# P times V in turns of three quarters behind every third softmax tile, in a fused attention and FP4-feed-forward layer on one core

## The reference

```python
qkv = (x @ w_qkv + b_qkv).reshape(b, n, 3, H, DH).transpose(2, 0, 3, 1, 4)
q, k, v = (qkv[0], qkv[1], qkv[2])
...
attn = jnp.einsum('bhqd,bhkd->bhqk', q, k) * scale
attn = jax.nn.softmax(attn, axis=-1)
out = jnp.einsum('bhqk,bhkd->bhqd', attn, v)
```

## Time and profile before

| | |
|---|---|
| median of 3 runs | 3654.96 us (3651.85 to 3660.76) |
| the profiled execution's own time | 3661.47 us |
| its span, first to last instruction | 3659.7 us |
| mean granted TensorE clock | 0.97 |
| TensorE matmul busy | 3412.5 us |
| VectorE busy | 3367.8 us |
| ScalarE busy | 2629.5 us |
| GpSimd busy | 911.9 us |

### The profile page before, as it was taken

How to read it: one execution, slowest core, us unless ns; L and a number is a source line. 1 busy time by engine, 2 the same in 40 slices (tenths; PEclk the granted TensorE clock), 3 DMA queues, 4 the chain that set the end, 5 groups by cost and what they waited for, 6 DMA issues and landing times.

```text
span 3659.7 us, 69024 instructions
## 1 busy us (share of the span) xinstructions
PE 3412.5 (93%) x27752; PEld 1539.9 (42%) x27752; DVE 3367.8 (92%) x3565; ACT 2629.5 (72%) x4870; POOL 911.9 (25%) x995
## 2 busy tenths in 40 slices
PE   7668999999999999999999999999999969999997
PEld 4343333333333333333333333333333336666665
DVE  8898999999999989999999999999999739999997
ACT  4342888888888888888888888888888833333333
POOL 6881000010000000000000000000000028888887
PEclk9885999999999999999999999999999989999999
DMA  5442112221211111111111111111111111211110
GB/s 162 144 168 89 57 66 72 74 69 65 73 57 47 55 61 67 58 41 43 50 61 61 59 61 48 41 41 62 63 67 52 46 42 46 79 42 39 40 34 21
DMA packets 134508, 230.63 MB, mean 63 GB/s; under 512 B 29510, under 2 KB 84006, under 8 KB 121894
## 3 DMA queue, kind: packets, MB, share of 16 engines
q1 hardware_dynamic: 124972, 217.82, 17.6%
q10 hardware_dynamic: 9216, 8.39, 0.7%
HBM read 156.33 MB, written 68.16 MB: 61 GB/s over the span
## 4 chain that ended last, share of the span: by engine, by line
PE 81%; DVE 9%; ACT 3%; issue 3%; DMA 1%; POOL 1%; SPq 1%; ACTq 0%; POOLq 0%; DVEq 0%
PE ps L625 36%; PE ps L678 32%; PE ps L758 7%; PE ps L768 4%; DVE arena L980 2%; DVE arena L985 1%; PE ps L728 1%; ACT arena L842 1%; PE ps L665 1%; ACT arena L851 1%; DVE arena L973 1%; DVE arena L1003 1%; ACT arena L889 0%; DMA qst<-qk_parts 0%; ACT v_all L899 0%
## 5 line engine op out<-in xcount | busy, mean ns | idle before, releaser
L1003 DVE TENSOR_REDUCE arena<-ps 128x1 f32<-128x1024 f32 x2048 | 2495.0, 1222 | 120.8 <-PE ps L625 103.9
L851 ACT ACTIVATE arena<-ps 128x512 f32<-128x512 f32 x4096 | 2226.1, 597 | 364.6 <-PE ps L665 280.0
L625 PE MATMUL ps<-kst,qst 48*128 48x512 f32 x4096 | 1522.1, 452 | 26.5 <-DMA qst<-qk_parts 22.2
L665 PE MATMUL ps<-qst,kst 51*128 51x512 f32 x4096 | 1494.4, 448 | 0.0
L678 PE MATMUL ps<-arena 128*32 128x256 f32 x16384 | 1312.2, 393 | 71.1 <-ACT arena L842 67.2
L625 PEld LDWEIGHTS ps<-kst,qst 48*128 48x128 f32 x4096 | 615.4, 188 | 886.0 <-DVE arena L1003 716.2
L678 PEld LDWEIGHTS ps<-arena 128*32 128x32 f32 x16384 | 326.7, 108 | 797.5 <-issue 459.8
L1259 POOL TENSOR_TENSOR arena<-arena,ones 128x16 bf16<-128x16 f32 x64 | 14.2, 221 | 2432.6 <-DVE arena L1008 2432.6
L665 PEld LDWEIGHTS ps<-qst,kst 51*128 51x128 f32 x4096 | 606.6, 185 | 11.1 <-ACT arena L851 7.7
L768 PE MATMUL ps<-wdT,arena 128*128 128x256 f32 (+1 forms) x768 | 195.0, 407 | 48.5 <-ACT arena L889 46.2
L899 ACT ACTIVATE v_all<-ps 128x352 f32<-128x352 f32 x128 | 59.3, 463 | 239.1 <-PE ps L758 238.9
(11 more groups left out here) (104 smaller groups left out, 2223.9 us busy)
## 6 DMA issues: line engine op xcount, KB each, us to landing
qk_parts<-arena SPq DMA_DIRECT2D x32, 1024.0 KB, 7.4
kst<-qk_parts SPq DMA_DIRECT2D x128, 256.0 KB
qst<-qk_parts SPq DMA_DIRECT2D x128, 256.0 KB
kst<-qk_parts SPq DMA_DIRECT2D x128, 128.0 KB
qst<-qk_parts SPq DMA_DIRECT2D x128, 128.0 KB
att<-arena SPq DMA_DIRECT2D x256, 34.0 KB
arena<-in_xT SPq DMA_DIRECT2D x16, 512.0 KB, 8.2
arena<-in_x SPq DMA_DIRECT2D x32, 256.0 KB
```

Source lines behind the costliest of these rows:

```text
L625: mm = nc.tensor.matmul(ps[:, i % S_BANKS, :], q[SROW:SROW + STACK, qt * P:(qt + 1) * P], k[SROW:SROW + STACK, kc * CHUNK:(kc + 1) * CHUNK ...
L665: nc.tensor.matmul(ps[:, bank_of_t(g.c, i), :], kst[g.u % 2][first:first + ROWS, kb * P:(kb + 1) * P], qst[g.u % 2][first:first + ROWS, qb ...
L851: nc.scalar.activation(pt[kb % 2][:, qb * CHUNK:(qb + 1) * CHUNK], ps[:, bank_of_t(g.c, i), :], ACT.Exp).then_inc(p_ready, 1)
L1003: nc.vector.tensor_reduce(mx[g.u % 2][:, i // 2, i % 2:i % 2 + 1], ps[:, bank:bank + 2, :].rearrange("p b t -> p (b t)"), AX.X, ALU.max).t ...
```

## The change

P times V is cut into quarters of 128 columns per block. Behind every third T tile (counted over all heads) come three quarters, sometimes four, or what is left of a head; a table `BEHIND` is made once by `products_behind`. Quarters of one block that stand together are one instruction per column group. `pt` gets a third buffer. ScalarE's copy of a head's output goes behind the exponential of the tile that its last quarters stand behind (`ENDS`), and `m_tile` goes behind tile 51, 52 or 53, the one that ends a run of three. S tiles are counted one by one. Where a run of three ends between the two S tiles of a pair, VectorE takes one maximum per bank (two reduces of 128 x 512) in place of one over both. The maxima of a head then need 4 columns per 128 queries in place of 2, and GpSimd sets them to the lowest float before each use.

```diff
-M_AFTER = 51
-
-HALF_AFTER = (1, 3)
+RUN, TILES_BACK = 3, 2
+QUARTERS, QUARTER = 4, 128
+
+MANY = 7
+
+P_BUFS = 3
+LOWEST = -3.4028234663852886e38
+
+M_FROM = 51
...
+def products_behind():
+
+    behind, done, head = {}, 0, KT * QUARTERS
+    for tile in range(G * TILES_S):
+        last_head = tile >= (G - 1) * TILES_S
+        if tile % RUN != RUN - 1 and not last_head or last_head and tile % CHUNKS != CHUNKS - 1:
+            continue
+        waiting = QUARTERS * max(0, (tile - TILES_BACK + 1) // CHUNKS) - done
+        count = waiting if last_head else min(waiting, QUARTERS if waiting >= MANY else QUARTERS - 1)
+        count = min(count, (done // head + 1) * head - done)
+        if count > 0:
+            behind[tile] = range(done, done + count)
+            done += count
+    return behind, range(done, G * head)
+
+
+BEHIND, AT_THE_END = products_behind()
+
+ENDS = {last.stop // (KT * QUARTERS) - 1: tile for tile, last in BEHIND.items() if last.stop % (KT * QUARTERS) == 0}
+
+
+def parted(g, pair):
+
+    beside = (g - 1) * TILES_S + 2 * pair - AHEAD
+    return beside >= 0 and beside % RUN == RUN - 1
+
+
+def m_after(g):
+
+    return M_FROM + (RUN - 1 - g * TILES_S - M_FROM) % RUN
...
-        mx = [take(KT * 2, "p (q c) -> p q c", c=2) for _ in range(2)]
+        mx = [sb(f"mx{i}", [P, KT, CHUNKS])[:, :, :] for i in range(2)]
...
-        pt = [take(N) for _ in range(2)]
+
+        pt = [take(N) for _ in range(P_BUFS - 1)] + [carve(12 * CHUNK + 16 * CHUNK)(N)]
...
-                pair = i // 2
                 if i == 0:
                     pe.wait_ge(s_in[g.u % 2], g.quad(128, 64 * (g.u // 2 + 1)))
-                if i % 2 == 0 and not (g.static(0) and pair < 2):
-                    pe.wait_ge(s_done, g.times(PAIRS, pair - 1))
+                wait_after(pe, s_done, g.times(TILES_S, i - S_BANKS + 1))
...
-                if i % 2:
-                    mm.then_inc(s_psum, 1)
+                mm.then_inc(s_psum, 1)
...
+            def pv(quarters):
+
+                g, first = divmod(quarters.start, KT * QUARTERS)
+                if first == 0:
+                    pe.wait_ge(v_staged, g + 1)
+                    wait_after(pe, o_out, g)
+                pe.wait_ge(p_ready, CHUNKS * ((quarters.stop - 1) // QUARTERS + 1))
+                at = quarters.start
+                while at < quarters.stop:
+                    block, q = divmod(at, QUARTERS)
+                    n = min(quarters.stop - at, QUARTERS - q)
+                    cols = slice(q * QUARTER, (q + n) * QUARTER)
+                    for qb in range(CHUNKS):
+                        mm = nc.tensor.matmul(ps[32 * qb:32 * qb + 32, O_BANK, cols], vs[g % 2][:, block % KT, :],
+                                              pt[block % P_BUFS][:, qb * CHUNK + cols.start:qb * CHUNK + cols.stop],
+                                              start=(block % KT == 0 and q == 0), stop=(block % KT == KT - 1 and q + n == QUARTERS))
+                    at += n
+                    if q + n == QUARTERS:
+                        mm.then_inc(pv_step, 1)
...
-                        halves = [HALF_AFTER.index(qb)] if qb in HALF_AFTER else []
-                        if g.static(G - 1):
-                            halves = [0, 1] if qb == CHUNKS - 1 else []
-                        for half in halves:
-                            if kb:
-                                pv(g, kb - 1, half)
-                            elif not g.static(0):
-                                pv(g.back(1), KT - 1, half)
+                        if g.c * TILES_S + kb * CHUNKS + qb in BEHIND:
+                            pv(BEHIND[g.c * TILES_S + kb * CHUNKS + qb])
...
-                    wait_after(act, pv_step, g.times(KT, kb - 1))
+                    wait_after(act, pv_step, g.c * KT + kb - P_BUFS + 1)
...
-                        if not g.static(0) and kb == 1 and qb == 0:
+                        if not g.static(0) and g.c * TILES_S + i == ENDS[g.c - 1]:
                             out_of_psum(g.back(1))
-                        if i == M_AFTER and not g.static(G - 1):
+                        if i == m_after(g.c) and not g.static(G - 1):
                             maxima(g.c + 1)
...
             def maxima(g):
+                dve.wait_ge(mx_clear, g.c + 1)
                 for i in range(PAIRS):
                     bank = 2 * i % S_BANKS
-                    dve.wait_ge(s_psum, g.times(PAIRS, i + 1))
-                    nc.vector.tensor_reduce(mx[g.u % 2][:, i // 2, i % 2:i % 2 + 1],
-                                            ps[:, bank:bank + 2, :].rearrange("p b t -> p (b t)"), AX.X, ALU.max
-                                            ).then_inc(s_done, 1)
+                    qt, kc = i // 2, i % 2 * 2
+                    if parted(g.c, i):
+                        for t in range(2):
+                            dve.wait_ge(s_psum, g.times(TILES_S, 2 * i + t + 1))
+                            nc.vector.tensor_reduce(mx[g.u % 2][:, qt, kc + t:kc + t + 1], ps[:, bank + t, :], AX.X, ALU.max
+                                                    ).then_inc(s_done, 1)
+                    else:
+                        dve.wait_ge(s_psum, g.times(TILES_S, 2 * i + 2))
+                        nc.vector.tensor_reduce(mx[g.u % 2][:, qt, kc:kc + 1],
+                                                ps[:, bank:bank + 2, :].rearrange("p b t -> p (b t)"), AX.X, ALU.max
+                                                ).then_inc(s_done, 2)
                     if i == PAIRS - 1:
-                        dve.wait_ge(s_done, g.times(PAIRS, i + 1))
+                        dve.wait_ge(s_done, g.times(TILES_S, TILES_S))
                         nc.vector.tensor_reduce(nm[g.u % 2], mx[g.u % 2], AX.X, ALU.max, negate=True).then_inc(neg_max, 1)
...
+            def clear_maxima(p):
+                nc.gpsimd.memset(mx[p], LOWEST).then_inc(mx_clear, 1)
...
                 p, first = g.u % 2, 3 * g.c
                 pool.wait_ge(neg_max, g.c + 1)
+                clear_maxima(p)
```

More of the change, by code:

```diff
@@ L140, in run_straight @@
                 fn(At(0, s - lag))
+def products_behind():
[18 more added lines that the diff above has]
+    return M_FROM + (RUN - 1 - g * TILES_S - M_FROM) % RUN
 def t_place(g, i):
-    return 1 + g * (TILES_S + 1) + i + (i > M_AFTER)
+    return 1 + g * (TILES_S + 1) + i + (i > m_after(g))
 def m_place(g):
-    return 0 if g == 0 else 1 + (g - 1) * (TILES_S + 1) + M_AFTER + 1
+    return 0 if g == 0 else 1 + (g - 1) * (TILES_S + 1) + m_after(g - 1) + 1
 def t_bank(place):
@@ L251, in layer_kernel @@
         bqk = take(4)
-        phase_a_end = arena_words - 2 * (2 * KT + 4 * KT)
+        phase_a_end = arena_words - 2 * 4 * KT
         WIDTHS = (6 * C, 6 * C, 2 * FF)
@@ L326, in layer_kernel @@
             "rot_ready", "rotsin", "t1_done", "qr_done", "hi_done", "parts_ready"))
-        s_psum, s_done, neg_max, m_step, m_split = (sem(n) for n in ("s_psum", "s_done", "neg_max", "m_step", "m_split"))
+        s_psum, s_done, neg_max, m_step, m_split, mx_clear = (sem(n) for n in (
+            "s_psum", "s_done", "neg_max", "m_step", "m_split", "mx_clear"))
         mt_psum, mt_out, t_psum, p_ready = (sem(n) for n in ("mt_psum", "mt_out", "t_psum", "p_ready"))
@@ L484, in head @@
                 if g < G - 2:
-                    sp.wait_ge(s_psum, bm * (8 * PAIRS) + (c + 1) * PAIRS)
+                    sp.wait_ge(s_psum, bm * (8 * TILES_S) + (c + 1) * TILES_S)
                     load_s(bm_s, (c + 2) % 8)
@@ L636, in t_bank_free @@
                 g, i = divmod(back - 1, TILES_S + 1)
-                if back == 0 or i == M_AFTER + 1:
+                if back == 0 or i == m_after(g) + 1:
                     pe.wait_ge(mt_out, 1 if back == 0 else g + 2)
                 else:
-                    pe.wait_ge(p_ready, g * TILES_S + i - (i > M_AFTER) + 1)
+                    pe.wait_ge(p_ready, g * TILES_S + i - (i > m_after(g)) + 1)
             def m_tile(g):
@@ L657, in t_tile @@
                 elif i < S_BANKS:
-                    pe.wait_ge(s_done, G * PAIRS)
+                    pe.wait_ge(s_done, G * TILES_S)
                 else:
@@ L695, in head @@
                         t_tile(g, kb, qb)
-                        if kb * CHUNKS + qb == M_AFTER and not g.static(G - 1):
+                        if kb * CHUNKS + qb == m_after(g.c) and not g.static(G - 1):
                             m_tile(g.c + 1)
-                        halves = [HALF_AFTER.index(qb)] if qb in HALF_AFTER else []
-                        if g.static(G - 1):
-                            halves = [0, 1] if qb == CHUNKS - 1 else []
-                        for half in halves:
-                            if kb:
-                                pv(g, kb - 1, half)
-                            elif not g.static(0):
-                                pv(g.back(1), KT - 1, half)
+                        if g.c * TILES_S + kb * CHUNKS + qb in BEHIND:
```

(17 more changed lines are left out.)

## The result

The changed kernel takes 3676.61 us (median of 5 runs, 3673.63 to 3678.05) against 3654.96 us: ratio 1.0054, interval 1.0039 to 1.0068. It is slower by some 20 us, where the forecast was 3632 us, faster by 23. The time lies inside the stated range (3560 to 3692) and on the other side of no change. One execution of the last experiment (13257 us) and one of the kernel before beside it (12867 us) were slow ones: they are in the medians given and left out of the ratios.

The account below looks back on a forecast made before the run. Bound: TensorE's 1.23 us turn for two tiles, plus a wait each head. The loop of waits, 40.48 + 0.14 - 0.20, gave 40.42 us a head against 40.79; over 63 heads 23 us, so 3655 becomes 3632 us (range 3560 to 3692).

Parts of the forecast that it names:

- What bounds the kernel before: Attention stage: TensorE's 1.23 us turn for two tiles, VectorE 0.10 us slack per pair, plus a 1.13 us head wait.
- (1) The boundary: Head's start: the wait around the output's copy and the 0.17 us go, all of 1.30 us a head.
- (2) The turns: TensorE: a third fewer turns to P times V; batch of three 0.79 us, twelve tiles 6.72 us against 7.40.
- One-bank reduces: VectorE, every third pair: two reduces of 128 x 512, each about 0.69 us long, the next starting 0.60 us later.
- Rival A: VectorE's one-bank reduces do not overlap, each taking 0.70 us: about 3698 us; chance 24%.
- The loop of waits: Twelve-tile chain through reduces, S tile 2, batches and tile 3's exponential: 7.59 us a round.
- the 0.76 us from tile 6 to the start of its reduce: Piece of the twelve-tile chain: tiles 6 and 7 to the start of their reduce on VectorE, 0.76 us.
- The transpose: Transpose of the maxima, once a head: stays but charged nothing; if uncovered, 0.17 us.
- The small terms: Maxima's reduce with the reciprocal adds 0.14 us a head; batches near head ends that don't wait take off 0.20.
- Rival B: The exponential's wait costs nothing: 38.9 us a head, about 3535 us; chance 20%.
- small loop of 3.63 us for six tiles: Loop through the banks alone, without the wait for the exponential: 3.63 us for six tiles.
- Rival C: Nothing moves that can be told: small costs left out stay uncovered, 0.37 us a head gone, 3655 us; chance 14%.

Follow-up runs that it names:

- the last experiment: Changed kernel with P times V three tiles back, semaphore raised by one per reduce, and the maxima's transpose behind the batch; 3567.52 us, ratio 0.9751.
- e6: Changed kernel with runs of two tiles and batches of two quarters, all its other parts kept; 3610.63 us, ratio 0.9873.
- e4: Kernel before with only ScalarE's output copy moved one tile earlier, behind the exponential of tile 3 instead of tile 4; 3604.78 us, ratio 0.9856.
- e2: Changed kernel with each reduce raising the semaphore by one and TensorE waiting on the number of reduces; 3649.93 us, ratio 0.9983.
- e5: Changed kernel with the maxima's transpose issued behind the batch of P times V instead of ahead of it; 3665.72 us, ratio 1.0023.
- e1: Changed kernel with P times V kept three tiles back instead of two; 3611.07 us, ratio 0.987.

## Why the prediction was wrong, point by point

The mechanism was forecast rightly; the sum was too small in three terms. A start that was priced without its separate wait gives 0.37 us a head, the transpose that was charged at nothing some 0.2, and batches of four quarters on the loop, not priced, 0.14. Together they are 0.7 us a head, twice the gain that the prediction had left (0.37).

- **What bounds the kernel before**: TensorE's turn of 1.23 us for two tiles with VectorE 0.10 us faster, and a wait at each head. Right: e6 and e4 keep 7.40 us for twelve tiles, and e4 shows that the head's wait, moved out of the way, is worth nearly its length.
- **(1) The boundary**: TensorE waits 0.6 us in the whole stage for the copy in the changed kernel. The new head's wait is gone, as forecast.
- **(2) The turns**: a batch of three quarters takes 0.78 to 0.79 us from its loads to the next tile's, and a third tile follows 0.23 us after the second. Both as forecast.
- **One-bank reduces**: 0.68 us long, 0.60 apart, as forecast. Rival A is refuted: they start 0.08 us before the one ahead has ended. The Trainium skill, "VectorE: DVE Perf Modes", section "The DRAIN you can't avoid", has the next operation wait for the empty pipe, but adds that one that isn't held starts earlier. The prediction's rival used the first half alone; the trace agrees with the second.
- **The loop of waits**: right in place and order, 7.66 against 7.59. **The term that was mis-sized is the 0.76 us from tile 6 to the start of its reduce. It measured 0.83** (503.37 to 504.20). The reduce now raises its semaphore by two and has its wait as an instruction of its own, where the prediction says only that S tiles counted singly are the same waits: I read it in the diff and did not price it. That is 0.07 in each round, 0.37 a head, 23 us; e2 took it away and gained 22 us by its heads and 27 by the medians. This term alone turns 3632 into about 3655, no change.
- **The transpose**: "I charge nothing for it" was wrong. I covered it by slack of TensorE, but the change moved it to the end of a run, where the bank that it takes was filled two tiles before. It waits 0.33 us every head, and it is itself a piece of the chain, between the exponential and the batch (1522.36 to 1522.71). By the rounds it costs some 0.2 us a head, 12 us. e5, which moves it but leaves it in the chain of one head in three, gives back 0.15, 10 us.
- **Batches of four quarters**: the table sends out four where seven or more wait, and all 62 such batches before the last head stand behind tile 5 of twelve. Of these, two in three heads wait for the exponential, and there the fourth quarter is on the loop: 1.07 us in place of 0.86, and rounds of 7.87 or 7.88 us, counted from tile 2 of twelve, in the changed kernel and in e5 alike. That is 0.14 us a head, 9 us, which the prediction, with every batch at 0.79, left out. It is read off the trace; no run took it away.
- **The small terms**: the maxima's reduce and the reciprocal lengthen two rounds in three heads, to 7.93 and 7.76 us counted the same way, 0.12 us a head where 0.14 was charged. Batches near a head's ends that do not wait give back 0.24 where 0.20 was taken off. Over three heads the sixteen rounds are 123.3 us where sixteen steady ones are 122.6; these two bullets and the transpose make up the difference.
- **Rival B** (3535 us if the exponential's wait cost nothing) was mis-sized: e1 took the wait away and reached 3611. I had put the small loop of 3.63 us for six tiles in its place, with no charge for the rounds near transpose and head's end. **Rival C** (small costs uncovered, 3655) named the right kind of error, with too small a sum: the transpose was uncovered, the clear was not (VectorE waited for it once in 39 heads, 0.3 us).

The gain at the head's boundary did not vanish: e6, the change without its runs of three, is some 46 us below the kernel before (3655 x 0.0127), as e4 is by 51 alone, and the runs of three took back 66. Taken away one at a time, the exponential's wait is worth 65 us, the wait instruction 27 and the transpose's place 11. Without all three the kernel takes 43 us less than e6.

## What to carry to other kernels

When an engine's turns are made rarer and longer, follow what each burst asks of its neighbours (banks, the newest result, the last reader's release): a distance of two tiles that was free in runs of two is a wait in runs of three. Price the largest burst where it stands on the path, and not the mean one. Look at the whole path through several engines and write it as one sum; the busy shares of all three engines of the stage fell here while the time rose. And when an edit changes how a semaphore is raised, look whether the wait still rides on its instruction, since a few hundredths of a microsecond on the path, 5 times in a head, were as large as the whole forecast gain.

## What the runs showed of the hardware

A VectorE reduce that raises its semaphore by two has its wait as an instruction of its own (DVEq L1047 in the chain) and starts 0.09 us behind TensorE's (modelled) end, where in e2 the same reduce raises by one and starts 0.02 us behind it. All 1379 pair reduces of the changed kernel have this row. Of its 1338 one-bank reduces, which raise by one, 21 have one. In e2 43 pair reduces and 21 one-bank reduces have one: together 64, as many as there are waits for the clear. Groups of P times V with 128 columns can follow each other 0.11 us apart (starts at 500.71 and 500.82 us), so that the weight loads of 32 columns stay covered even there.
